# Constant lag of the first experts' result scatters, router scatters in two of three tiles, last stage with its products three steps ahead

## The chip, the cores and the metric

The kernel runs on one core of one Trainium2 chip. The core has five engines: TensorE (PE in the profile; PEld are its weight loads), VectorE (DVE), ScalarE (ACT), GpSimd (POOL) and SyncE (SP, which here only starts transfers). The metric is the device time of one execution in microseconds; lower is better.

## The reference

The input is 16 sequences of 512 tokens with 128 features, float32. A mixture of experts, an attention and the same mixture of experts again are added to it, the first and the last with the factor one half:

```python
x = L0_attn_x
x = x + 0.5 * ffn(_layernorm(x)); x = x + attn(_layernorm(x)); x = x + 0.5 * ffn(_layernorm(x))

def ffn(x):                      # top 2 of 8 experts, and a shared one
    normed = (xt - mu) * rsqrt(var + eps) * ln_gamma + ln_beta
    probs = softmax(normed @ router_w.T);  top_v, top_i = top_k(probs, 2);  gates = softmax(top_v)
    out = sum over the two chosen experts e of gate_e * swiglu(normed, gate_up_w[e], down_w[e])
    return out + swiglu(normed, shared_gate_up_w, shared_down_w)
# swiglu(h, gu, down) = (silu(h @ gate.T) * (h @ up.T)) @ down.T
```

The attention has 16 heads of 8 features and a relative position term. All of its work stands between the two places that are changed.

## The kernel before

The 8192 tokens lie in SBUF all the time as `XR`, 64 groups of 128 tokens; four groups are a step (16 steps). The program has four blocks, each ended by a barrier over all engines: `route` (routing and the experts of the first mixture), `combine`, `attention` (attention, with routing of the second mixture, and then its experts) and `finish`.

**Experts (route and attention).** POOL scatters the normalized rows to a table in HBM, `dispatched`, sorted by expert (indirect DMAs, 128 rows each). Then 71 tiles (`ET`) of 256 rows are worked off. SP loads a tile's rows up to eight tiles ahead. PE transposes them (`s_tx`), ACT copies them out, DVE splits them in high and low parts (the cast to `Xh`, L636 and L1814, is one per tile), PE makes gate and up products (`x_gu`), ACT the silu, DVE the product, PE the down product (`x_dn`), DVE copies the result out (`s_y`, L650 and L1825), and POOL scatters it with two indirect DMAs to `expert_out` in HBM (L400 and L1421). The order within each engine is the order in which the code is written; an engine goes on when the semaphores of its next instruction are there. The result buffers form a ring of 24 tiles.

POOL's scatters of tile n are bound to PE's progress. In the attention block the first waits for the gate and up products of tile n + 2 (`x_gu` at n + 3), the second for the transposes of tile n + 4. In `route` the number 3 was `lag = max(3, 15 - n // 4)`: 15 tiles at first, one less every fourth tile, 3 from tile 48 on:

```python
                q, y, lag = n % 4, n % YR, max(3, 15 - n // 4)
                    if g == 0:
                        pool.wait_ge(x_gu, min(ET, n + lag))
                    else:
                        pool.wait_ge(s_tx, min(ET, n + lag + 2))
```

In the attention block POOL also has 16 router scatters left for the last two batches (`send`, L1408). From tile `LATE` = 13 on it put one between a tile's two result scatters, in 16 tiles in a row. SP waits for all of them before it loads the rows of tile 48 and later.

**The end of the attention block.** POOL waits until its scatters have landed (L1472), and so does SP (L1355), which then loads the experts' results of steps 0 and 1 (L1359). Behind each engine's last instruction the block has a drain (L1161 in the profile) and then the barrier.

**The last stage (finish), per step.** SP loads both experts' results (`Y`, two DMAs of 256 KB, L2064). POOL scales one and adds the residual (L2082, L2084). ACT normalizes three groups (L2128) and DVE the fourth (L2091). PE transposes them (L2149), ACT applies gamma and beta (L2136), PE makes the shared expert's gate (L2158) and up (L2159), ACT the silu (L2140), DVE the hidden product (L2103), PE the down product (L2164). DVE adds the gated results (four instructions, L2098, "gated sum") and then the shared expert's (L2108), and SP stores the step (L2074). PE's down product follows its gate product by one step; `h` has two buffers.

Of the kernel before, what the change touches and what calls it, by code (L numbers as in the profile page):

```python
# [12 lines left out]
ALU = mybir.AluOpType  # L13
# [3 lines left out]
P = 128  # L17
# [127 lines left out]
def build(nc, T):  # L145
    with ExitStack() as top:
# [47 lines left out]
        with ExitStack() as c:  # L194
            R = gates(K, c, "f2", None)
            attention(K, "f2", R)
            finish(K, "f2", R)

# [19 lines left out]
def route(K, tag, R):  # L218
# [11 lines left out]
    with ExitStack() as c:  # L230
# [147 lines left out]
        def _(pool):  # L378
# [778 lines left out]
def attention(K, tag, R2):  # L1157
# [3 lines left out]
    with ExitStack() as c:  # L1161
# [94 lines left out]
        s_st = [SX(f"out{q}") for q in range(4)]  # L1256
# [34 lines left out]
        def _(sp):  # L1291
# [62 lines left out]
            for q in range(4):  # L1354
                sp.wait_ge(s_st[q], 16 * NG2 * ((ET - q + 3) // 4))  # L1355
            yv = yd[0:TOPK * TOK, :].rearrange("(k n p) d -> p k n d", k=TOPK, p=P)
            for s in range(2):
                for k in range(TOPK):
                    sp.dma_start(R2["Y"][s][k], yv[:, k, tokens(s), :]).then_inc(R2["s_ga"][s], 16)  # L1359

        @block.gpsimd
        def _(pool):
# [108 lines left out]
            for q in range(4):  # L1471
                pool.wait_ge(s_st[q], 16 * NG2 * ((ET - q + 3) // 4))  # L1472
# [560 lines left out]
def finish(K, tag, R):  # L2033
# [6 lines left out]
    with ExitStack() as c:  # L2040
        Y = R["Y"] + [[sb(c, f"{tag}_Y{q}{k}", [P, JT, D]) for k in range(TOPK)] for q in range(2, NB)]
        xn = [sb(c, f"{tag}_xn{q}", [P, JT, D]) for q in range(3)]
        nT, sg, h = ([sb(c, f"{tag}_{x}{q}", [P, L]) for q in range(2)] for x in ("nT", "sg", "h"))
# [3 lines left out]
        s_ga = R["s_ga"]  # L2047
        s_st = S("stored")
        s_n, s_nv, s_tp, s_nT, s_gu, s_sg, s_h, s_dn, s_pa, s_cb, s_out = (
            S(x) for x in ("normed", "normed_dve", "transp", "nT", "gateup", "silu", "hidden", "down", "second", "first", "shared"))  # L2050
        block = c.enter_context(nc.Block())
        JA = JT - 1
# [5 lines left out]
        def _(sp):  # L2058
# [7 lines left out]
            for s in range(2, 5):  # L2066
                wait(sp, (s_cb, JT * (s - 3)))
                load(s)
# [18 lines left out]
        def _(dve):  # L2087
            def normalize(s):
                t = JT * s + JA
                wait(dve, (s_tp, s - 2))  # L2090
                nc.vector.tensor_scalar(xn[s % 3][:, JA, :], XR[:, t, :], rstd[:, t:t + 1], shift[:, t:t + 1], ALU.mult, ALU.add  # L2091
                                        ).then_inc(s_nv, 1)

# [7 lines left out]
            def hidden(s):  # L2101
                wait(dve, (s_sg, s + 1), (s_gu, s + 1), (s_dn, s - 1))
                nc.vector.tensor_tensor(h[s % 2][:], psU[s % 2][:], sg[s % 2][:], ALU.mult).then_inc(s_h, 1)  # L2103
# [19 lines left out]
        def _(act):  # L2123
            def normalize(s):
                wait(act, (s_tp, s - 2))
                for j in range(JA):
# [6 lines left out]
            for s in range(NB + 1):  # L2133
                if s < NB:
                    wait(act, (s_tp, s + 1), (s_gu, s - 1))
                    nc.scalar.activation(nT[s % 2][:], psT[s % 2][:], ACT.Identity, bias=bet[:], scale=gam[:]).then_inc(s_nT, 1)  # L2136
                if s >= 1:
                    b = s - 1
                    wait(act, (s_gu, b + 1), (s_h, b - 1))
                    nc.scalar.activation(sg[b % 2][:], psG[b % 2][:], ACT.Silu).then_inc(s_sg, 1)  # L2140
# [4 lines left out]
        def _(pe):  # L2145
            def transposes(s):
                wait(pe, (s_n, JA * (s + 1)), (s_nv, s + 1), (s_nT, s - 1))
# [5 lines left out]
            for s in range(NB + 1):  # L2153
                if s + 1 < NB:
                    transposes(s + 1)
                if s < NB:
                    wait(pe, (s_nT, s + 1), (s_sg, s - 1), (s_h, s - 1))
                    nc.tensor.matmul(psG[s % 2][:], sgT[:], nT[s % 2][:], start=True, stop=True)  # L2158
                    nc.tensor.matmul(psU[s % 2][:], suT[:], nT[s % 2][:], start=True, stop=True).then_inc(s_gu, 1)  # L2159
                if s >= 1:  # L2160
                    b = s - 1
                    wait(pe, (s_h, b + 1), (s_out, b - 1))
                    for j in range(JT):
                        m = nc.tensor.matmul(psY[b % 2][:, j, :], h[b % 2][:, j * P:(j + 1) * P], sdT[:], start=True, stop=True)  # L2164
# [51 lines left out]
```

## Time and profile before

| | us |
|---|---|
| median of 3 runs (lowest to highest) | 2274.42 (2271.9 to 2279.68) |
| profiled execution | 2267.75 |
| its span | 2265.8 |
| first experts, 71 tiles | about 217 to 506 |
| second experts, 71 tiles | about 1885 to 2182 |
| last stage | 2197.4 to 2265.8 |

TensorE is busy 2055.6 us of the span (91%), DVE 1849.0 (82%), ACT 1351.1 (60%), POOL 1336.5 (59%). These are means over stages with different limits. In the first experts' stage TensorE sets the pace where it is busy all of a window; in the last stage DVE is the engine that is hardly idle.

### The profile page before, as it was taken

The page shows a single profiled execution, that of the slowest core. Times are in us where ns is not written, and L with a number is a line of the kernel's source. Part 1 is how long each engine was busy: PE and PEld are TensorE (multiplying, and loading weights), DVE is VectorE, ACT ScalarE, POOL GpSimd, SP SyncE. Part 2 cuts the span into 40 slices and gives each one's busy share as a digit, 9 for nine tenths or more (in the row PEclk, how much of TensorE's full clock was granted, in tenths as well). Part 3 has the DMA queues.
Part 4 walks back from the last instruction along what each step waited for, and adds up shares of the span by engine and source line. Part 5 has one row for each costly group of instructions (what it writes and reads, how often), then busy time and mean ns, then how long its engine had stood idle before and what let it go on. Part 6 is the DMA issues. An engine that isn't in the chain of part 4 may idle for free. (4 is left out here: it accounts for less than half of the span.)

```text
span 2265.8 us, 64247 instructions
## 1 busy us (share of the span) xinstructions
PE 2055.6 (91%) x22864; PEld 1244.0 (55%) x22865; DVE 1849.0 (82%) x3842; ACT 1351.1 (60%) x3301; POOL 1336.5 (59%) x1961
## 2 busy tenths in 40 slices
PE   7664988996799999999999999999999997889968
PEld 4443988893344444444444444444444447889965
DVE  6543755667699999999999999999999995666648
ACT  4332544556766766666677667667666655445545
POOL 3665155553355557757757667667577583465554
PEclk8666999999999999999999999999999999999989
DMA  5222242217801111210111011012102104232226
GB/s 158 75 67 84 64 151 88 73 50 232 209 13 34 34 26 19 45 34 13 43 34 45 11 38 49 4 39 48 34 12 44 40 24 156 60 89 74 68 63 185
DMA packets 161414, 149.02 MB, mean 66 GB/s; under 512 B 51602, under 2 KB 135698, under 8 KB 160594
## 3 DMA queue, kind: packets, MB, share of 16 engines
q1 hardware_dynamic: 141984, 109.36, 18.6%
q0 software_dynamic: 17280, 35.56, 4.8%
q8 instruction: 163, 2.67, 0.5%
q14 instruction: 113, 0.93, 0.1%
q10 hardware_dynamic: 1874, 0.51, 0.1%
HBM read 86.76 MB, written 62.55 MB: 66 GB/s over the span
## 5 line engine op out<-in xcount | busy, mean ns | idle before, releaser
L1521 PE MATMUL ps_scores<-c_relw,arena_stats 64*64 64x512 f32 x4096 | 956.5, 598 | 0.0
L1972 ACT ACTIVATE arena_probs<-ps_scores,neg_max 128x512 f32<-128x512 f32 x1024 | 697.0, 684 | 393.6 <-DVE neg_max L1857 389.7
L1857 DVE TENSOR_REDUCE neg_max<-ps_scores 128x1 f32<-128x512 f32 x1024 | 650.0, 662 | 26.9 <-PE ps_scores L1521 24.6
L1509 PE MATMUL ps_scores<-arena_rows,arena_stats 64*64 64x512 f32 x2048 | 483.6, 598 | 5.6 <-ACT arena_probs L1972 3.7
L1509 PE MATMUL ps_scores<-c_batch,arena_stats 64*64 64x512 f32 x2048 | 475.3, 596 | 4.7 <-POOL arena_stats L1449 2.6
L1521 PEld LDWEIGHTS ps_scores<-c_relw,arena_stats 64*64 64x64 f32 x4096 | 277.0, 132 | 247.3 <-issue 185.1
L1654 DVE STREAM_TRANSPOSE arena_weights<-arena_probs 128x1024 f32<-128x1024 f32 x256 | 313.5, 1224 | 1.8 <-ACT arena_probs L1972 1.8
L1654 DVE STREAM_TRANSPOSE arena_results<-arena_probs 128x1024 f32<-128x1024 f32 x256 | 313.2, 1224 | 0.0
L1447 POOL TENSOR_TENSOR arena_stats<-arena_rows,c_mask 128x128 f32<-128x128 f32 x256 | 121.9, 476 | 193.2 <-PE ps_scores L1521 191.6
L1447 POOL TENSOR_TENSOR arena_stats<-c_batch,c_mask 128x128 f32<-128x128 f32 x256 | 121.5, 475 | 193.5 <-PE ps_scores L1521 192.3
L1421 POOL DMA_INDIRECT expert_out<-arena_results,f2x_to x142 | 139.4, 982 | 120.8 <-PE ps_scores L1577 73.7
L1972 ACT ACTIVATION_READ_ACCUMULATOR arena_probs<-ps_scores,neg_max 128x1 f32 x1024 | 200.3, 196 | 0.0
L1509 PEld LDWEIGHTS ps_scores<-c_batch,arena_stats 64*64 64x64 f32 x2048 | 136.2, 132 | 106.8 <-issue 86.4
L1509 PEld LDWEIGHTS ps_scores<-arena_rows,arena_stats 64*64 64x64 f32 x2048 | 132.1, 132 | 111.2 <-issue 93.4
L1373 POOL TENSOR_TENSOR row_recip<-row_sum,minus_one 128x16 f32<-128x16 f32 x64 | 186.6, 2916 | 8.2 <-ACT arena_probs L1972 8.2
L390 POOL DMA_INDIRECT dispatched<-f1d_n,f1d_idx x128 | 124.5, 973 | 90.9 <-DVE f1d_idx L542 48.9
L400 POOL DMA_INDIRECT expert_out<-f1d_n,f1x_to x94 | 91.1, 969 | 66.4 <-PE f1d_bank L955 24.2
L1588 PE MATMUL ps_values<-c_batch,arena_results 128*128 x852 | 110.9, 281 | 19.7 <-issue 10.8
L953 PE MATMUL f1d_bank<-f1x_Xh,f1x_Th 128*128 128x256 f32 x426 | 127.1, 298 | 0.2 <-issue 0.2
L1575 PE MATMUL ps_scores<-f2x_Xh,f2x_Th 128*128 128x256 f32 x426 | 126.1, 296 | 1.1 <-DVE f2x_Xl L1818 0.9
L966 PE MATMUL f1d_bank<-f_Wd,f1d_act 128*128 x852 | 108.5, 277 | 17.2 <-DVE f1d_n L650 13.5
L955 PE MATMUL f1d_bank<-f1x_Xh,f1x_Tl 128*128 128x256 f32 x426 | 121.1, 284 | 0.5 <-issue 0.5
(323 smaller groups left out, 4225.9 us busy)
## 6 DMA issues: line engine op xcount, KB each, us to landing
qkv_record<-f1c_rec SPq DMA_DIRECT2D x16, 768.0 KB, 3.9
c_batch<-dispatched SPq DMA_DIRECT2D x71, 129.0 KB
arena_rows<-dispatched SPq DMA_DIRECT2D x71, 129.0 KB
c_batch<-qkv_record SPq DMA_DIRECT2D x32, 256.0 KB
arena_rows<-qkv_record SPq DMA_DIRECT2D x32, 256.0 KB
f2c_Y<-expert_out SPq DMA_DIRECT2D x28, 256.0 KB, 3.3
c_Os<-expert_out SPq DMA_DIRECT2D x20, 256.0 KB, 4.1
f1c_Y<-expert_out SPq DMA_DIRECT2D x16, 256.0 KB, 4.3
```

Source lines behind the costliest of these rows:

```text
L390: pool.indirect_dma_start(xd, bass.IndirectOffsetOnAxis(idx[:, k, t:t + 1], 0), n0[k][s % NR][:, j, :], None).then_inc(s_sc[s % 4], 16)
L953: nc.tensor.matmul(dst, wh, Xh[q][:], start=True, stop=False)
L955: m = nc.tensor.matmul(dst, wl, Xh[q][:], start=False, stop=True)
L1373: tt(rr[:, G % 2, :], rs[:, G % 2, :], minus[:], ALU.pow).then_inc(s_rr, 1)
L1421: pool.indirect_dma_start(yd, bass.IndirectOffsetOnAxis(to[y][:, g:g + 1], 0), Ys[y][:, g, :], None).then_inc(s_st[q], 16)
L1447: tt(SK[u % NS], qk, mk, ALU.mult).then_inc(s_ex, 1)
L1509: m = nc.tensor.matmul(out, SK[n // 2 % NS][p, h, :, :].rearrange("p h a -> p (h a)"), KT[q][p, h, :], start=True, stop=False)
L1521: m = nc.tensor.matmul(out, SR[n // 2 % NS][p, h, :, :].rearrange("p h a -> p (h a)"), R[p, w0:w0 + L], start=False, stop=True)
L1575: nc.tensor.matmul(dst, wh, Xh[q][:], start=True, stop=False)
L1654: nc.vector.transpose(PT[G % 2][:, :, 2 * pair:2 * pair + 2, :, :].rearrange("p r i h a -> p r (i h a)"), Pr[U % NPAIR].rearrange("p i (r ...
L1857: reduce_max(nmx[U % NPAIR][:, n % 2:n % 2 + 1], psS[U % NPAIR][n % 2][:], AX, negate=True).then_inc(s_mx, 1)
L1972: nc.scalar.activation(Pr[s][:, n % 2, :], psS[s][n % 2][:], ACT.Exp, bias=nmx[s][:, n % 2:n % 2 + 1], accum_out=rs[:, G % 2, tt:tt + 1]). ...
```

## The change

`route`: the lag is 3 from the first tile. `attention`: the 16 router scatters go into two of every three tiles; POOL and SP no longer wait at its end for the result scatters, and SP no longer loads steps 0 and 1 there. The semaphores of these scatters now live on into `finish`, where SP waits for them behind the barrier and then loads all steps. `finish`: ACT normalizes all four groups, `h` has four buffers, PE's down product is three steps behind its gate product, and DVE makes the hidden products three steps ahead. The small buffers lie in one piece, `early`.

```diff
@@ route, POOL @@
-                q, y, lag = n % 4, n % YR, max(3, 15 - n // 4)
+                q, y = n % 4, n % YR
-                        pool.wait_ge(x_gu, min(ET, n + lag))
+                        pool.wait_ge(x_gu, min(ET, n + 3))
-                        pool.wait_ge(s_tx, min(ET, n + lag + 2))
+                        pool.wait_ge(s_tx, min(ET, n + 5))
@@ attention, SP @@
-            for q in range(4):
-                sp.wait_ge(s_st[q], 16 * NG2 * ((ET - q + 3) // 4))
-            yv = yd[0:TOPK * TOK, :].rearrange("(k n p) d -> p k n d", k=TOPK, p=P)
-            for s in range(2):
-                for k in range(TOPK):
-                    sp.dma_start(R2["Y"][s][k], yv[:, k, tokens(s), :]).then_inc(R2["s_ga"][s], 16)
@@ attention, POOL @@
-                        if 0 <= n - LATE < TOPK * JP:
-                            send(LASTP, n - LATE)
+                        at = n - LATE
+                        if at >= 0 and at % 3 < 2 and at // 3 * 2 + at % 3 < TOPK * JP:
+                            send(LASTP, at // 3 * 2 + at % 3)
-            for q in range(4):
-                pool.wait_ge(s_st[q], 16 * NG2 * ((ET - q + 3) // 4))
@@ finish @@
-        JA = JT - 1
+        HB, AHEAD_H, ROWS = 4, 3, TR // P
@@ finish, SP @@
-            for s in range(2, 5):
+            for q in range(4):
+                sp.wait_ge(s_rows[q], 16 * ROWS * ((ET - q + 3) // 4))
+            for s in range(5):
                 wait(sp, (s_cb, JT * (s - 3)))
                 load(s)
@@ finish, DVE @@
-            for s in range(2):
-                normalize(s)
-            for s in range(NB + 1):
-                if s + 2 < NB:
-                    normalize(s + 2)
-                if s < NB:
-                    hidden(s)
-                    gated(s)
-                if s >= 1:
-                    shared(s - 1)
+            for s in range(AHEAD_H):
+                hidden(s)
+            for s in range(NB):
+                gated(s)
+                if s + AHEAD_H < NB:
+                    hidden(s + AHEAD_H)
+                shared(s)
@@ finish, ACT @@
-                for j in range(JA):
+                for j in range(JT):
@@ finish, PE @@
-            for s in range(NB + 1):
+            for s in range(NB + AHEAD_H):
-                if s >= 1:
-                    b = s - 1
+                if s >= AHEAD_H:
+                    b = s - AHEAD_H
                     wait(pe, (s_h, b + 1), (s_out, b - 1))
```

In `route` no instruction changes its place, only what it waits for. POOL in the second experts' stage, from tile 13's first result scatter (`expert_out`) on, before; `dispatched` is a router scatter:

```order
L1421 DMA expert_out<-arena_results,f2x_to 20224x128
L1408 DMA dispatched<-f_n,f_idx 69376x129
L1421 DMA expert_out<-arena_results,f2x_to 20224x128 x2
L1408 DMA dispatched<-f_n,f_idx 69376x129
L1421 DMA expert_out<-arena_results,f2x_to 20224x128 x2
```

The same place now:

```order
L1417 DMA expert_out<-arena_results,f2x_to 20224x128
L1403 DMA dispatched<-f_n,f_idx 69376x129
L1417 DMA expert_out<-arena_results,f2x_to 20224x128 x2
L1403 DMA dispatched<-f_n,f_idx 69376x129
L1417 DMA expert_out<-arena_results,f2x_to 20224x128 x4
```

After every second router scatter there are now four result scatters instead of two.

SP from the last row load of the experts to the loads of the last stage, before (`f2x_out` counts landed result scatters):

```order
L1304 DMA arena_rows<-dispatched 128x2x129
L1359 DMA c_Os<-expert_out 128x4x128 [waits f2x_out2,f2x_out3,f2x_out1,f2x_out0]
L1359 DMA c_Os<-expert_out 128x4x128 x3
L1161 UNCONDITIONAL_BRANCH
L2057 UNCONDITIONAL_BRANCH [waits barrier_Pool_Activation_PE_DVE_SP_release]
L2064 DMA f2c_Y<-expert_out 128x4x128 x4
```

The same place now:

```order
L1305 DMA arena_rows<-dispatched 128x2x129
L1162 UNCONDITIONAL_BRANCH
L2054 UNCONDITIONAL_BRANCH [waits barrier_Pool_Activation_PE_DVE_SP_release]
L2061 DMA c_Os<-expert_out 128x4x128 [waits f2x_out2,f2x_out3,f2x_out1,f2x_out0]
L2061 DMA c_Os<-expert_out 128x4x128 x3
L2061 DMA f2c_Y<-expert_out 128x4x128 x4
```

The wait for the scatters and the four loads have moved behind the barrier.

DVE at the start of the last stage, before (`xn` is the fourth group's normalization, `h` the hidden product):

```order
L2091 TENSOR_SCALAR f2c_xn<-residual,c_rs,c_shift 128x128 x3
L2103 TENSOR_TENSOR f2c_h<-f2c_psup,f2c_sg 128x512
L2098 SCALAR_TENSOR_TENSOR c_Os<-c_Os,f_gate 128x128 x4
L2091 TENSOR_SCALAR f2c_xn<-residual,c_rs,c_shift 128x128
L2103 TENSOR_TENSOR f2c_h<-f2c_psup,f2c_sg 128x512
```

The same place now (`early` holds the hidden tiles):

```order
L2096 TENSOR_TENSOR f2c_early<-f2c_psup,f2c_early 128x512 x3
L2091 SCALAR_TENSOR_TENSOR c_Os<-c_Os,f_gate 128x128 x4
L2096 TENSOR_TENSOR f2c_early<-f2c_psup,f2c_early 128x512
L2101 SCALAR_TENSOR_TENSOR c_Os<-f2c_psY,c_Os 128x512
L2091 SCALAR_TENSOR_TENSOR c_Os<-c_Os,f_gate 128x128 x4
```

Three hidden products stand ahead of the first gated sum, and DVE's normalizations are gone.

## Rows read from the trace of the kernel before

**Rows 1.** Windows of all engines: us, busy (x instructions), PE clock, DMA share, GB/s.

```profile
227.00:256.00 29.00, 29.00 (x253) 29.00 (x252) 24.46 (x78) 16.48 (x31) 0.00 (x0) 1.00 0.20 52
...
286.00:440.00 154.00, 137.08 (x1132) 133.61 (x1131) 89.76 (x246) 72.47 (x141) 91.08 (x95) 0.99 0.32 105
...
440.00:498.00 58.00, 58.00 (x504) 58.00 (x503) 40.27 (x112) 33.11 (x64) 30.65 (x32) 1.00 0.19 56
...
2230.00:2251.00 21.00, 18.66 (x97) 12.53 (x96) 20.84 (x43) 14.56 (x31) 12.94 (x12) 1.00 0.75 220
```

**Rows 2.** Windows, the first experts' casts alone (L636, one per tile).

```profile
286.00:439.80 153.80, 10.28 (x35) 0.99 0.32 105
439.80:498.30 58.50, 4.70 (x16) 1.00 0.19 56
```

**Rows 3.** Windows of the second experts' stage: all engines, then casts alone (L1814).

```profile
1962.00:2034.00 72.00, 60.24 (x484) 56.77 (x483) 44.05 (x131) 31.40 (x61) 45.05 (x47) 1.00 0.29 85
...
1962.00:2034.00 72.00, 4.48 (x16) 1.00 0.29 85
...
2040.00:2178.00 138.00, 10.90 (x37) 1.00 0.22 65
```

**Rows 4.** Timeline of one slow tile: start us, us, engine line op [idle before].

```profile
1986.19 0.42 DVE L1825 COPY arena_results<-ps_values 128x256 f32<-128x256 f32 x1 [1.01 <-remote]
...
1986.48 0.95 POOL L1421 DMA_INDIRECT expert_out<-arena_results,f2x_to  x1 [1.15 <-PE ps_scores L1577]
...
1987.74 0.96 POOL L1421 DMA_INDIRECT expert_out<-arena_results,f2x_to  x1 [0.30 <-issue]
...
1988.31 0.38 PE L1560 MATMUL ps_side<-ident,arena_rows 128*128 128x128 f32 x2
...
1989.00 0.96 POOL L1408 DMA_INDIRECT dispatched<-f_n,f_idx  x1 [0.31 <-issue]
...
1990.84 0.42 DVE L1825 COPY arena_results<-ps_values 128x256 f32<-128x256 f32 x1 [1.02 <-remote]
```

**Rows 5.** The barriers: POOL's last scatter, its two drains, ACT's first.

```profile
2185.67 0.96 POOL L1421 DMA_INDIRECT expert_out<-arena_results,f2x_to  x1 [0.30 <-issue]
...
L1161 POOLq DRAIN  x1: 8971/8971/8971, 2188.2 to 2188.2; - x1
...
L230 POOLq DRAIN  x1: 2844/2844/2844, 513.0 to 513.0; - x1
...
2197.47 1.65 ACT L2128 ACTIVATE f2c_xn<-residual,c_shift,c_rs 128x128 f32<-128x128 f32 x4 [16.44 <-PEq L1161]
```

**Rows 6.** Timeline: the first hidden product, two waits, DVE's last instructions.

```profile
2205.13 0.69 DVE L2103 TENSOR_TENSOR f2c_h<-f2c_psup,f2c_sg 128x512 f32<-128x512 f32 x1 [4.20 <-ACT f2c_sg L2140]
...
2211.68 1.04 POOL L2082 TENSOR_TENSOR f2c_Y<-f2c_Y,f_gate 128x512 f32<-128x512 f32 x1 [4.80 <-DMA f2c_Y<-expert_out]
...
2217.56 0.81 PE L2149 MATMUL f2c_psT<-ident,f2c_xn 128*128 128x128 f32 x4 [3.10 <-issue]
...
2261.48 1.28 DVE L2108 SCALAR_TENSOR_TENSOR f2c_Y<-f2c_psY,f2c_Y 128x512 f32<-128x512 f32 x2
```

**Rows 7.** Groups of 2230:2251 (busy, mean ns), then L2098, L2082, L2084 (ns).

```profile
L2098 DVE SCALAR_TENSOR_TENSOR f2c_Y<-f2c_Y,f_gate 128x128 f32<-128x128 f32 x25 | 12.8, 569 | 0.0
...
L2128 ACT ACTIVATE f2c_xn<-residual,c_shift,c_rs 128x128 f32<-128x128 f32 x18 | 7.5, 483 | 0.0
...
L2091 DVE TENSOR_SCALAR f2c_xn<-residual,c_rs,c_shift 128x128 f32<-128x128 f32 x6 | 2.2, 374 | 0.0
...
L2098 DVE SCALAR_TENSOR_TENSOR f2c_Y<-f2c_Y,f_gate x56: 336/342/1426, 2211.8 to 2261.2; 128x128 f32<-128x128 f32 x56
...
L2082 POOL TENSOR_TENSOR f2c_Y<-f2c_Y,f_gate x14: 1038/1040/1221, 2202.2 to 2253.0; 128x512 f32<-128x512 f32 x14
...
L2084 POOL TENSOR_TENSOR f2c_Y<-f2c_Y,residual x14: 1262/1268/1289, 2203.3 to 2254.1; 128x512 f32<-128x512 f32 x14
```

**Rows 8.** The page's DMA issues: count, KB each, median us to landing.

```profile
f2c_Y<-expert_out SPq DMA_DIRECT2D x28, 256.0 KB, 3.3
```

More of the change, by code:

```diff
@@ L195, in build @@
             R = gates(K, c, "f2", None)
+            R["s_st"] = [c.enter_context(nc.semaphore(f"f2x_out{q}")) for q in range(4)]
             attention(K, "f2", R)
@@ L1255, in attention @@
         s_ld = [SX(f"in{q}") for q in range(4)]
-        s_st = [SX(f"out{q}") for q in range(4)]
+        s_st = R2["s_st"]
         s_tx, s_xf, s_hl, x_gu, x_sg, x_h, x_dn, s_y, s_wl, s_to = (
@@ L2040, in finish @@
     with ExitStack() as c:
+        early = sb(c, f"{tag}_early", [P, 11 * L])
+        homes = [early[:, q * L:(q + 1) * L] for q in range(11)]
+        xn = [home.rearrange("p (j d) -> p j d", j=JT) for home in homes[0:3]]
+        nT, sg, h = homes[3:5], homes[5:7], homes[7:11]
+        assert 11 * L * 4 <= 49152
         Y = R["Y"] + [[sb(c, f"{tag}_Y{q}{k}", [P, JT, D]) for k in range(TOPK)] for q in range(2, NB)]
-        xn = [sb(c, f"{tag}_xn{q}", [P, JT, D]) for q in range(3)]
-        nT, sg, h = ([sb(c, f"{tag}_{x}{q}", [P, L]) for q in range(2)] for x in ("nT", "sg", "h"))
         psT, psG, psU = ([ps(c, f"{tag}_ps{x}{q}", [P, L]) for q in range(2)] for x in ("T", "gate", "up"))
@@ L2046, in finish @@
         S = Sems(nc, c, tag)
-        s_ga = R["s_ga"]
+        s_ga, s_rows = R["s_ga"], R["s_st"]
         s_st = S("stored")
-        s_n, s_nv, s_tp, s_nT, s_gu, s_sg, s_h, s_dn, s_pa, s_cb, s_out = (
-            S(x) for x in ("normed", "normed_dve", "transp", "nT", "gateup", "silu", "hidden", "down", "second", "first", "shared"))
+        s_n, s_tp, s_nT, s_gu, s_sg, s_h, s_dn, s_pa, s_cb, s_out = (
+            S(x) for x in ("normed", "transp", "nT", "gateup", "silu", "hidden", "down", "second", "first", "shared"))
         block = c.enter_context(nc.Block())
-        JA = JT - 1
+        HB, AHEAD_H, ROWS = 4, 3, TR // P
         def tokens(s):
@@ L2087, in _ @@
         def _(dve):
[L2088 to L2092, printed above, removed]
             def gated(s):
@@ L2101, in hidden @@
             def hidden(s):
-                wait(dve, (s_sg, s + 1), (s_gu, s + 1), (s_dn, s - 1))
-                nc.vector.tensor_tensor(h[s % 2][:], psU[s % 2][:], sg[s % 2][:], ALU.mult).then_inc(s_h, 1)
+                wait(dve, (s_sg, s + 1), (s_gu, s + 1), (s_dn, s + 1 - HB))
+                nc.vector.tensor_tensor(h[s % HB], psU[s % 2][:], sg[s % 2], ALU.mult).then_inc(s_h, 1)
             def shared(s):
@@ L2135, in _ @@
                     wait(act, (s_tp, s + 1), (s_gu, s - 1))
-                    nc.scalar.activation(nT[s % 2][:], psT[s % 2][:], ACT.Identity, bias=bet[:], scale=gam[:]).then_inc(s_nT, 1)
+                    nc.scalar.activation(nT[s % 2], psT[s % 2][:], ACT.Identity, bias=bet[:], scale=gam[:]).then_inc(s_nT, 1)
                 if s >= 1:
@@ L2139, in _ @@
                     wait(act, (s_gu, b + 1), (s_h, b - 1))
-                    nc.scalar.activation(sg[b % 2][:], psG[b % 2][:], ACT.Silu).then_inc(s_sg, 1)
+                    nc.scalar.activation(sg[b % 2], psG[b % 2][:], ACT.Silu).then_inc(s_sg, 1)
                 if s + 2 < NB:
@@ L2146, in transposes @@
             def transposes(s):
-                wait(pe, (s_n, JA * (s + 1)), (s_nv, s + 1), (s_nT, s - 1))
+                wait(pe, (s_n, JT * (s + 1)), (s_nT, s - 1))
                 for j in range(JT):
```

6 lines of the change are left out of this document (3 added, 3 removed).

## The prediction

> **What bounds the kernel now.** I read the windows by stage first, then the starts of one instruction per tile, then the wait rows, and last the end of the program. The attention middle keeps TensorE (PE) busy and the change does not touch it, so only three places matter.
>
> *First experts' stage, tiles 19 to 54.* The window 286 to 440 us has PE busy 137.08 of 154 us, while 227 to 256 and 440 to 498 have it busy all the time [rows 1]. VectorE (DVE) casts each tile's rows once, so its casts count tiles: 35 in 153.8 us, 4.39 us each, then 16 in 58.5 us, 3.66 us each [rows 2]. What differs is GpSimd (POOL). It issues 95 scatters in the slow window, 2.7 a tile, and 32 in the fast one, 2 a tile [rows 1], because its lag of 15 tiles shrinks by one tile every fourth, so it does four tiles' scatters while PE does three.
>
> *Second experts' stage.* The same again: 16 tiles in 72 us with 47 scatters, three each (two results, one router scatter), and 37 tiles in 138 us (3.73 us) where the code has two each [rows 3]. The rows of one slow tile show how it costs [rows 4]. Three scatters start at 1986.48, 1987.74 and 1989.00. PE's transposes are over at 1988.69 and the down matmuls of which the DVE copy waits came before them, yet the copy starts only at 1990.84, 1.84 us after the third scatter began. PE's signals are passed on late behind a run of three scatters. Why, the rows do not say; the price is the difference: this tile's copy starts 4.65 us after the one before it (1986.19), a free one 3.71, so 0.94 us for each third scatter.
>
> *The end.* POOL's last scatter starts at 2185.67. What then holds the block's barrier is POOL's drain, 8.971 us from 2188.2; ACT starts at 2197.47, so the barrier opens at about 2197.4. The same drain took 2.844 us behind the first experts [rows 5]. Then the last stage runs 68.4 us to the span's end at 2265.8. In its middle (2230 to 2251) DVE is busy 20.84 of 21 us over six steps, so a step is 3.50 us and DVE is its limit [rows 1, 7].
>
> **The first experts' scatters, three tiles behind.** With a constant lag POOL starts at tile 3 and issues two scatters a tile throughout. The 35 slow tiles then go at the fast pace. I take 3.70 us, between the 3.66 of [rows 2] and the 3.73 of [rows 3]: 153.8 - 35 x 3.70 = 24.3 us gained, all on the path, since PE bounds the stage and the tail (lag 3 from tile 48 on) is the same in both. Nothing is queued on POOL at that point: it is idle in the window 227 to 256 [rows 1]. The 24 scatters that move to tiles 3 to 14 come beside DVE at 24.46 of 29 us [rows 1], the only place with this rate that the trace does not show. Bounds: nothing there, and 3.66 us a tile, gives 25.7; every one of these 12 tiles held at 0.94 us gives 24.3 - 11.3 = 13.0.
>
> **The 16 router scatters of the second stage, in two of three tiles.** There are still 16 tiles with a third scatter, spread over 23. If each costs 0.94 us, nothing changes: 15.0 before and after. The first stage's regime had the same eight scatters in three tiles and cost (3 x 4.39 - 3 x 3.71) / 2 = 1.0 us for each extra one, so +1 us at worst. If POOL's rate were the limit instead (4.65 / 3 = 1.55 us a scatter), 62 scatters take 96.1 us against 23 x 3.71 = 85.3, that is 10.8 in place of 15.0, a gain of 4.2. I take 0, by the row nearest in kind. The row loads that wait for the last of these start at tile 41, three tiles behind the last send's turn, so they stay hidden.
>
> **The barrier.** POOL no longer waits for its scatters to land, so its drain starts at 2186.65 instead of 2188.2. With the same 8.97 us the barrier opens 1.6 us sooner. If the drain ends when it ended before, 0; if it takes the 2.844 us of the other block, 7.7. I take 1.6. SP's four loads of steps 0 and 1, which lay under the drain, now come behind the barrier. They land in 3.3 us [rows 8] and POOL needs 2.3 us for a step's two operations (1040 and 1268 ns [rows 7]), so step 0 is ready for DVE some 6 us behind it. What hides that is the new order itself: DVE now makes three hidden tiles before its first gated sum.
>
> **The last stage.** The first hidden tile started 7.7 us after the barrier (2205.13) [rows 6]. ScalarE (ACT) now makes the fourth normalization of a step too, two of them before its first product: +0.8. It is busy 14.56 us in six steps [rows 1], 2.4 a step, and with one more at 0.4 it needs 2.8 (18 normalizations took 7.5 us [rows 7]). So the third hidden tile ends at 7.7 + 0.8 + 2 x 2.8 + 0.6 = 14.7 us, and here the first gated sum starts. Before, it started at 8.3: the lookahead costs 6 us at the front. From there DVE has per step 3.50 less the removed normalization (2.2 us in six, 0.37 each [rows 7]) = 3.13; PE was busy 18.66 us in six steps, 3.1 each [rows 1]. The first four steps find POOL ahead and follow PE at 3.1 (12.4 us; no load is awaited, for four steps' loads go out at once, where before POOL stood 4.80 us until 2211.68 for one, and PE 3.10 us until 2217.56 [rows 6]), nine go at 3.15 (28.4), the last three have no hidden tile and a free POOL, 1.9 each (5.7), and from DVE's last operation to the end 3.0 us as now (2262.8 to 2265.8 [rows 6]). Sum 14.7 + 12.4 + 28.4 + 5.7 + 3.0 = 64.2 against 68.4: 4.2 gained. Bounds: a front of 13.0 (ACT at 2.4 a step) and 13 steps at PE's 3.1 give 62.0 (6.4 gained); all 13 steps at today's 3.50, because loads and stores are the limit at the 220 GB/s of [rows 1], give 68.9 (0.5 lost).
>
> How much POOL slows DVE decides the 3.13. A gated sum takes 336 ns at best and up to 1426 [rows 7], just over POOL's 1268, and 25 of them took 12.8 us, 2.05 a step, not 1.1. I keep the 2.05, since POOL's work for a step is not touched. Were POOL's part gone, a DVE step would be 2.2 and PE's 3.1 would bound nine steps, 0.5 us less in the sum. The Trainium skill, "SBUF — State Buffer", section "Who interferes with whom", says that a VectorE instruction with two SBUF inputs and a GpSimd one that reads SBUF exclude each other for the whole instruction. The trace agrees: the longest gated sum is 1090 ns over the shortest, about one POOL operation. By this rule the sum stays at 64.2; if POOL's work cost DVE nothing, it would be 63.7.
>
> **Sum.** 24.3 + 0 + 1.6 + 4.2 = 30.1 us. The profiled execution took 2267.75 us with a span of 2265.8; it goes to about 2237.7. The median of the runs is 2274.42, 6.7 above it, and I carry that over: **2244.3 us**.
>
> **Rivals.**
> - *Early tiles are held as well* (12%). Two scatters beside a fuller DVE hold PE's signals in tiles 3 to 14: 13.0 + 5.8 gained, 2255.6. For it: the one place without a row. Against it: the fast windows have the same pair of scatters and PE busy throughout.
> - *The drain shrinks* (8%). 2.844 us as behind the first experts: 24.3 + 7.7 + 4.2, 2238.2. For it: one of two drains measured. Against: the code behind and ahead of this barrier is unchanged.
> - *The last stage gives nothing* (11%): DMA-bound steps and the 6 us front: 24.3 - 0.5, 2250.6. For it: 0.75 of the DMA engines' time in the middle. Against: the loads now run four steps ahead.
> - *The slow window was never about scatters* (4%), but say the DMA traffic, 105 GB/s there against 52 and 56 [rows 1]. Then only the 5.8 us at the end are left: 2268.6, no change. Against: the second stage slows the same way with three scatters at 85 GB/s [rows 3], and there the extra traffic is the third scatter's own.
> - *Slower* (3%): two scatters a tile hold PE's signals wherever DVE is late, in all of tiles 3 to 54. Each held tile costs 0.94, so 52 cost 48.9 against the 24.3 + 5.8 taken away: 2293.2. It decides from 33 held tiles on. Against: tiles 55 to 70 and 37 tiles of the second stage show none.
>
> **How the numbers follow.** The likeliest case holds 62%, with its own range 2239 to 2250. The 80% range leaves out the slower case, most of the no-change one and the tail of a short drain: 2235 to 2257. A measurement of this kernel can tell 0.3%, 6.8 us: faster 0.93 (the likeliest and the first three rivals), within 0.3% 0.04, slower 0.03.
>
> **What would show it.** Right: casts in the first experts' stage at 3.7 us from tile 5 to 70, no scatter run longer than two there, PE busy all of 240 to 495 us; second stage's slow stretch as long in sum; POOL's drain near 9 us; three hidden tiles before the first gated sum, steps of about 3.1 us, stage near 64 us. Wrong: casts beyond 4 us apart with two scatters a tile, or a last stage as long as 68 us.

## The result, and the profile after

The changed kernel took 2248.19 us (median of 4 runs, 2248.01 to 2249.22) against 2276.82 for the kernel before (4 runs, 2271.9 to 2279.68): a ratio of 0.9877, 95% interval 0.9857 to 0.9898, or 28.6 us. Forecast was 2244.3 us. The two profiled executions differ by less, 2265.8 to 2246.2 us of span, 19.6 us: the one of before (2267.75 us) was 4.2 us shorter than the shortest of its timed runs, and the one of after (2248.01 us) is an average one. The sections below count with the traces first and come back to the rest.

**First experts' stage.** The windows of the cast that stands once in each tile (L637 now), answering to [rows 2]; columns are the window, its length, DVE's time in this line with its count, PE clock, DMA share, GB/s:

```profile
291.40:421.20 129.80, 10.30 (x35) 1.00 0.35 111
226.60:291.40 64.80, 4.98 (x17) 0.94 0.30 90
421.20:480.70 59.50, 4.86 (x17) 1.00 0.19 57
```

The 35 tiles that took 153.8 us take 129.8, 3.71 each. All engines in the same window (PE, PEld, DVE, ACT, POOL), answering to the slow window of [rows 1]:

```profile
291.40:421.20 129.80, 129.80 (x1123) 129.80 (x1122) 88.73 (x245) 72.16 (x140) 67.32 (x70) 1.00 0.35 111
```

PE is never idle, and POOL issues 70 scatters, two a tile. Not all of the 24 us is kept. Tile 2 starts at 226.7 in place of 224.3, ahead of anything that the lag could move, and from tile 2 to tile 19 the starts of the cast stand 64.8 us apart, where they stood 62.1 apart before. These 2.7 us lie in tiles 2 to 5 alone; from tile 5 on the pace is the same as before, with two scatters a tile. All engines in tiles 2 and 3 now, and in tile 2 before:

```profile
226.70:231.50 4.80, 3.94 (x16) 3.43 (x17) 3.16 (x12) 2.06 (x4) 0.00 (x0) 0.50 0.19 50
231.50:235.70 4.20, 4.20 (x29) 4.20 (x28) 3.31 (x13) 2.17 (x4) 1.49 (x2) 0.70 0.41 110
```

```profile
224.30:227.70 3.40, 3.40 (x32) 3.40 (x31) 3.06 (x12) 2.12 (x4) 0.00 (x0) 1.00 0.29 83
```

Tile 2 runs at the low level of PE's granted clock (0.50, 1.2 GHz); before, the clock was at the high one (1.00, 2.4 GHz) there. In the 7.6 us ahead of tile 2 PE was busy 2.93 us now and all the time before. The first result scatter starts at 233.38, behind tile 2, so at least 1.4 of the 2.7 us are not the new lag's.

**Second experts' stage.** The 23 tiles from tile 17 to tile 40, before and after, all engines:

```profile
1961.60:2061.90 100.30, 88.54 (x728) 85.07 (x728) 64.65 (x187) 47.76 (x92) 60.38 (x62) 1.00 0.28 82
```

```profile
1944.10:2045.30 101.20, 89.21 (x735) 85.93 (x735) 64.62 (x186) 48.37 (x92) 60.28 (x62) 1.00 0.28 81
```

The same 62 scatters in nearly the same time, however they are spread. The other first-chip traces of the next section widen this: 102.6 and 103.8 us with the old order (end_only, lag_only), 100.8 and 100.9 with the new one (router_only, fours).

**The barrier.** POOL's last scatter, its drain (ns) and ACT's first instruction, answering to [rows 5]:

```profile
2167.86 0.95 POOL L1417 DMA_INDIRECT expert_out<-arena_results,f2x_to  x1 [0.30 <-issue]
...
L1162 POOLq DRAIN  x1: 11198/11198/11198, 2166.1 to 2166.1; - x1
...
2177.57 0.88 ACT L2118 ACTIVATE f2c_early<-residual,c_shift,c_rs 128x128 f32<-128x128 f32 x2 [14.34 <-PEq L1162]
```

The drain now reads 11.2 us because it is entered before the last scatters have run; it ends at 2177.3, 9.4 us after the last scatter started. Before it ended at 2197.2, 11.5 us after. That is 2.1 us gained. In the other traces from this chip it ends 11.5 and 11.1 us after that start with POOL's wait for the landings (lag_only, router_only), and 9.9 and 9.5 without it (end_only, fours).

**The last stage.** From the end of the drain to the end of the span it takes 68.9 us, and took 68.6. DVE's first hidden tile and first gated sums (start, us, engine, line, idle before):

```profile
2185.57 0.69 DVE L2096 TENSOR_TENSOR f2c_early<-f2c_psup,f2c_early 128x512 f32<-128x512 f32 x1 [19.31 <-ACT f2c_early L2130]
...
2191.54 1.13 DVE L2091 SCALAR_TENSOR_TENSOR c_Os<-c_Os,f_gate 128x128 f32<-128x128 f32 x4
...
2236.83 2.14 DVE L2091 SCALAR_TENSOR_TENSOR f2c_Y<-f2c_Y,f_gate 128x128 f32<-128x128 f32 x4
```

The order is the planned one: three hidden tiles, then the first gated sum 14.2 us behind the barrier. The row at 2236.83 is the fourteenth step's gated sums, so 13 steps took 45.3 us, 3.48 each. In parts, by the starts of the gated sums (us, from the end of the drain):

| | before | after |
|---|---|---|
| to the first gated sum | 8.5 | 14.2 |
| the first 4 steps | 16.3 | 13.1 |
| the next 9 steps | 32.6 | 32.2 |
| from there to the end | 11.2 | 9.4 |

The later front is paid back, all but 0.3 us, by the first four steps, which now find hidden tiles ready, and by the end. The nine steps between, 3.63 us each before and 3.58 now, are about as long as they were, although each has lost a normalization. The groups of 2210 to 2231 (line, busy us, mean ns), answering to [rows 7], show where it went:

```profile
L2091 DVE SCALAR_TENSOR_TENSOR f2c_Y<-f2c_Y,f_gate 128x128 f32<-128x128 f32 x24 | 15.7, 711 | 0.0
```

A gated sum takes 711 ns, and took 569. By the traces the parts of the 19.6 us are: +23.7 in tiles 19 to 54, -2.4 at tile 2, -2.7 from there to tile 19, -0.7 behind tile 54, -0.3 from there to the second experts' last tile, +2.3 up to the barrier (2.1 of it behind the last scatter) and -0.3 in the last stage, 19.6 in all.

### The profile page after: what moved, and what is told of

It reads as the page before. It is cut to its first block and busy times, and to the rows that moved or that the text cites. A ratio compares the mean times of both kernels' runs of the same rounds, so it can differ in the third digit from the quotient of the medians.

```text
span 2246.2 us, 64242 instructions
## 1 busy us (share of the span) xinstructions
PE 2052.5 (91%) x22864; PEld 1242.0 (55%) x22865; DVE 1844.7 (82%) x3826; ACT 1356.8 (60%) x3317; POOL 1336.8 (60%) x1961
## 5 line engine op out<-in xcount | busy, mean ns | idle before, releaser
L1582 PE MATMUL ps_values<-c_batch,arena_results 128*128 x852 | 111.2, 281 | 19.6 <-DVE arena_results L1819 10.8
L955 PE MATMUL f1d_bank<-f1x_Xl,f1x_Th 128*128 128x256 f32 x426 | 121.6, 285 | 0.0
```

Source lines behind the costliest of these rows:

```text
L955: nc.tensor.matmul(dst, wh, Xl[q][:], start=False, stop=False)
```

## The experiments

They ran in three sets, and each set beside runs of the kernel before on its own chip. That turned out to matter: before took 2275.5 us in the first set, like the result's 2276.8, but 2131.7 and 2131.8 in the second and third. Ratios are within a set.

### Set one: which part of the change gives the time

**lag_only** is the kernel before with this alone:

```
-                q, y, lag = n % 4, n % YR, max(3, 15 - n // 4)
+                q, y = n % 4, n % YR
...
-                        pool.wait_ge(x_gu, min(ET, n + lag))
+                        pool.wait_ge(x_gu, min(ET, n + 3))
...
-                        pool.wait_ge(s_tx, min(ET, n + lag + 2))
+                        pool.wait_ge(s_tx, min(ET, n + 5))
```

> The kernel before with only the first experts' lag set to three tiles. My theory (a third scatter back to back holds PE's signals, about 2 us for each of the runs of four in tiles 19 to 54): the whole of the stage's gain is here, 18 us by the two profiles shown and up to the 24 predicted, so 2250 to 2257 us, and the casts of tiles 19 to 54 stand 3.7 us apart. Rival (the gain is mostly in the end of the program or in the router scatters): under 5 us.

2253.6 us (2252.02 to 2255.18), ratio 0.9899 (0.9881 to 0.9917), 21.9 us of 2275.5. Its casts of tiles 19 to 54:

```profile
291.20:420.90 129.70, 10.30 (x35) 1.00 0.34 111
```

**end_only** is the changed kernel with the lag and the router scatters of before, so it has the missing wait at the end of attention, the loads moved and the new last stage.

> The changed kernel with the first experts' lag and the router scatters as before: only the end of the attention block and the last stage are changed. By the profiles: about 2 us from the barrier (POOL's landing wait gone, drain as long as it was) and nothing from the last stage (68.7 us against 68.4), so 0.998 to 1.000 of the time before. The prediction's own terms were 1.6 + 4.2 = 5.8 us. Rival (the last stage gains and the trace of after is an odd one): 6 us and a last stage of 64 us.

2272.99 us, ratio 0.9989 (0.9975 to 1.0002), 2.5 us and not clear of zero. The last stage is 68.6 us again, and the casts of tiles 19 to 54, with the old lag, are slow:

```profile
290.70:442.90 152.20, 10.69 (x35) 1.00 0.33 105
```

**router_only** is the kernel before with this alone:

```
-                        if 0 <= n - LATE < TOPK * JP:
-                            send(LASTP, n - LATE)
+                        at = n - LATE
+                        if at >= 0 and at % 3 < 2 and at // 3 * 2 + at % 3 < TOPK * JP:
+                            send(LASTP, at // 3 * 2 + at % 3)
```

> The kernel before with only the router scatters sent in two of three tiles. If each third scatter costs its own 0.94 us: no change, casts over tiles 17 to 40 in 100 us, as one stretch of 16 slow and 7 free tiles was. Rival (POOL's rate is the limit, so that spreading pays): 4 us faster. Rival (a tile behind two crowded ones loses too): 2 to 4 us slower.

2273.49 us, ratio 0.9992 (0.9982 to 1.0002): no change that can be told, and tiles 17 to 40 took 100.8 us. A loss of 2 to 4 us is excluded by the interval; a gain of 4 us lies at its very edge (0.9982 is 4.1 us). The parts give 21.9, 2.5 and 2.0, in all 26.4 of the 28.6 us, and only the first is clear of zero: the lag is about four fifths of the change.

**fours** changes only when POOL issues the two-a-tile scatters of the changed kernel:

```
-                    if g == 0:
-                        pool.wait_ge(x_gu, min(ET, n + 3))
-                    else:
-                        pool.wait_ge(s_tx, min(ET, n + 5))
+                    if n % 2 == 0 and g == 0:
+                        pool.wait_ge(x_gu, min(ET, n + 4))
+                        pool.wait_ge(s_tx, min(ET, n + 6))
```

> The changed kernel, but in the first experts' stage POOL waits until both tiles of a pair are due and then issues their four scatters in one run: still two a tile, but runs of four instead of two. If runs of three and more hold PE's signals, each run costs what the run of four cost in the slow window of before, 3 x (4.39 - 3.71) = 2.0 us, so 33 runs cost 60 to 70 us and the program takes about 2310. Rival (only the rate counts, 2.7 scatters a tile were too many for POOL or the DMA): no loss, 2248.

2300.07 us in one run, 52 above the changed kernel. So on this chip it is the run of scatters and not their rate. Its timeline (start, us, engine, line, idle before):

```profile
329.25 0.96 POOL L400 DMA_INDIRECT expert_out<-f1d_n,f1x_to  x1 [4.36 <-DVE f1d_n L650]
...
330.51 0.96 POOL L400 DMA_INDIRECT expert_out<-f1d_n,f1x_to  x1 [0.30 <-issue]
...
331.78 0.96 POOL L400 DMA_INDIRECT expert_out<-f1d_n,f1x_to  x1 [0.30 <-issue]
...
333.04 0.96 POOL L400 DMA_INDIRECT expert_out<-f1d_n,f1x_to  x1 [0.31 <-issue]
335.01 0.42 DVE L650 COPY f1d_n<-f1d_bank 128x256 f32<-128x256 f32 x1 [2.73 <-remote]
335.06 0.56 ACT L820 ACTIVATE c_batch<-f1d_bank,beta_col,gamma_col 128x256 f32<-128x256 f32 x1 [2.82 <-remote]
...
335.69 1.60 PE L966 MATMUL f1d_bank<-f_Wd,f1d_act 128*128 x12 [1.40 <-DVE f1d_n L650]
```

DVE and ACT, which both wait for PE, start together 1.97 and 2.02 us after the fourth scatter began, and then PE waits for DVE. In tiles 19 to 54 (the casts L636 here) the stage took 160.4 us, so a pair of tiles costs 1.7 us more than with runs of two, where 2.0 were expected:

```profile
302.30:462.70 160.40, 10.29 (x35) 1.00 0.29 93
```

### Set two: the last stage

Four variants of the changed kernel, to find what keeps the step at 3.5 us. **dve_norm** gives DVE the fourth normalization back (not shown: the first five of them ahead of the loop, ACT's loop over three groups, PE's wait for both):

```
+            def normalize(s):
+                t = JT * s + JT - 1
+                wait(dve, (s_tp, s - 2))
+                nc.vector.tensor_scalar(xn[s % 3][:, JT - 1, :], XR[:, t, :], rstd[:, t:t + 1], shift[:, t:t + 1], ALU.mult, ALU.add
+                                        ).then_inc(s_nv, 1)
...
                gated(s)
+                if s + AHEAD_H + 2 < NB:
+                    normalize(s + AHEAD_H + 2)
```

> The changed kernel, but DVE makes the fourth normalization of each step again, as before; the order with three hidden tiles ahead stays. The last stage of the changed kernel took 68.9 us from the end of POOL's drain, at 3.5 us a step, though DVE lost 0.37 us of work a step: its gated sums went from 2.05 to 2.6 us a step. Theory 1 (a gated sum and a POOL operation, both on SBUF alone, do not run together: a step is POOL's 2.31 plus the gated sums' 1.13, 3.44 us, and DVE's other work fits beside POOL's): the stage becomes at most 1 to 2 us longer. Theory 2 (DVE's own sum of work bounds the step and the 0.37 was really saved, something else having grown): 13 steps of 0.37, 4 to 5 us longer.

**quarter** and **half** move one or two of a step's four token tiles from POOL to DVE (JG is 3 or 2; not shown: POOL's operations over JG tiles only, and DVE's wait for POOL, which now stands behind these lines):

```
+                for j in range(JG, JT):
+                    t = JT * s + j
+                    nc.vector.scalar_tensor_tensor(out=Y[s][1][:, j, :], in0=Y[s][1][:, j, :], scalar=G2[:, t:t + 1],
+                                                   in1=XR[:, t, :], op0=ALU.mult, op1=ALU.add).then_inc(s_pd, 1)
```

> The changed kernel, but of each step's four token tiles in the last stage one is multiplied and added by DVE (one more operation of 0.3 us a step) and POOL keeps three. Theory 1 (POOL's operations and the gated sums exclude each other): 1.73 of POOL plus 1.43 of DVE is 3.16 a step in place of 3.44, the stage 3 to 4 us shorter. Theory 2 (DVE's work is the sum, POOL's share of the slowing fixed): 0.3 us a step longer, 4 to 5 us. Theory 3 (loads and stores at 217 GB/s bound the step): no change, 3.5 us a step.

> The same with two of four token tiles moved from POOL to DVE. Theory 1: 1.16 of POOL plus 1.73 of DVE exclude each other, 2.9; DVE alone needs 3.1 and PE 3.1, so the step is 3.1 to 3.2 and the stage 4 to 5 us shorter than 68.9. Theory 2: 8 to 9 us longer. Theory 3: no change.

**ahead1** has one hidden tile ahead:

```
-        HB, AHEAD_H, ROWS = 4, 3, TR // P
+        HB, AHEAD_H, ROWS = 4, 1, TR // P
```

> The changed kernel, but with one hidden tile made ahead in place of three; ACT still normalizes all four. The first gated sum starts some 6 us earlier (8 us behind the barrier in place of 14). If the step stays bound by POOL and the gated sums at 3.5 us, that time comes back but for the waits the lookahead hid: the stage 2 to 6 us shorter than 68.9. If the lookahead is what keeps PE and DVE supplied (my prediction): the steps get longer and the stage stays at 68 to 69 us.

Medians 2130.30, 2129.98, 2129.72 and 2127.14 us; ratios to before 0.9994 (0.9985 to 1.0004), 0.9990 (0.9980 to 1.0000), 0.9987 (0.9977 to 0.9997) and 0.9980 (0.9971 to 0.9990). From the end of the drain to the end the stage took 69.9, 69.8, 69.7 and 66.4 us; the changed kernel's own on these chips is 69.4 (set three). dve_norm is 0.5 us longer in all, and not 4 to 5. This is a sum of two: ACT, with less to do, lets the first gated sum start 1.9 us sooner, and the first four steps take 2.1 us more. The nine steps behind them take 32.6 us against 32.5 in the changed kernel (set three), and they are the test: a normalization more on DVE costs nothing there, as theory 1 has it. Taking POOL's work away and giving it to DVE costs nothing, and gains nothing either. Theory 1 had 3 to 5 us here and is missed; no change is what theory 3 forecast, and set three tries that. In half DVE's additional operation took 576 ns, not 300, in spite of the smaller POOL part, and PE was busy 20.62 of 21 us:

```profile
2085.00:2106.00 21.00, 20.62 (x104) 13.63 (x103) 20.38 (x51) 18.36 (x40) 8.24 (x12) 1.00 0.78 227
```

```profile
L2091 DVE SCALAR_TENSOR_TENSOR f2c_Y<-f2c_Y,f_gate,residual 128x128 f32<-128x128 f32 x12 | 6.4, 576 | 0.0
```

ahead1 is the best of the complete kernels here. Its first gated sum starts 5.4 us sooner than in the changed kernel. The first four steps, without hidden tiles in store, take 16.2 us in place of 12.9, the nine behind them 30.8 in place of 32.5, and the end 0.7 more. Expected was that longer steps would take the whole of the 5.4 us back; the steps and the end took 2.4.

### Set three: before and after on such a chip, POOL gone, the DMA loaded

**before_again** and **after_again** are the two kernels themselves.

> The kernel before, unchanged, profiled beside the next three. The four kernels of the last comparison ran on another chip, where before took 2131.7 us and the kernels with the new lag 2127 to 2130: there the traces show three and four scatters back to back with casts still 3.7 us apart. If that is the chip, this kernel there has no slow window in tiles 19 to 54 (35 tiles in about 130 us) though its lag still shrinks; on the first chip it has one (151 to 158 us). Rival (the gain was never from the lag): the slow window is there and the changed kernel lacks it, with the same total.

> The changed kernel, unchanged, as the base of the last stage on the same chip. From the end of POOL's drain to the end 68.9 us on the first chip. If chips don't differ in this stage: 68.9 here too. Against before: 0.9877 on the first chip; where runs of scatters hold nothing, only the barrier is left, 2 us, 0.999.

**no_pool** leaves out, for the last stage, POOL's two operations and DVE's wait for them (not shown), so the second gate and the residual are missing from its result:

```
-                nc.gpsimd.tensor_tensor(y, y, G2[:, tokens(s)].unsqueeze(2).broadcast_to([P, JT, D]), ALU.mult).then_inc(s_pa, 1)
-                wait(pool, (s_pa, 2 * s + 1))
-                nc.gpsimd.tensor_tensor(y, y, XR[:, tokens(s), :], ALU.add).then_inc(s_pa, 1)
```

> The changed kernel with POOL's two operations a step left out of the last stage (the second gate and the residual are not applied). Theory 1 (POOL's operations stretch DVE's gated sums): gated sums 0.34 us each, DVE needs 2.5 us a step, PE 3.1, so the step falls from 3.5 to 3.1 and the stage by 5 us. Theory 3 (loads and stores of 768 KB a step at 220 GB/s bound it): the step stays at 3.5 and DVE waits for loads.

**extra_store** writes each result twice (not shown: the last wait counts both):

```
                 sp.dma_start(ov[:, tokens(s), :], Y[s][1][:]).then_inc(s_st, 16)
+                sp.dma_start(xv2[:, tokens(s), :], Y[s][1][:]).then_inc(s_st, 16)
```

> The changed kernel with each step's result stored a second time, to another place in memory: 1024 KB a step in place of 768. Theory 3 (the DMA's rate bounds the step): 3.5 becomes 4.6 us and the stage 13 to 17 us longer. Theory 1 (POOL and DVE bound it, the DMA engines at three quarters have room): at most 2 us, for the last store.

The kernel before took 2130.98 us, the changed one 2129.88: ratios to the shared runs of before 1.0001 (0.9992 to 1.0011) and 0.9991 (0.9982 to 1.0001). The change that gave 28.6 us gives 1 to 2 here, and not clear of zero. The casts of tiles 19 to 54 in before_again, and all engines in the same window:

```profile
194.20:323.90 129.70, 11.55 (x35) 1.00 0.43 138
```

```profile
194.20:323.90 129.70, 129.70 (x1122) 129.70 (x1121) 90.88 (x246) 74.49 (x141) 99.11 (x100) 1.00 0.43 138
```

The old lag, 100 scatters in 35 tiles, more DMA traffic than on the first chip, and no loss: 129.7 us, as with the new lag. One piece of its timeline:

```profile
254.65 0.96 POOL L400 DMA_INDIRECT expert_out<-c_Os,f1x_to  x1 [0.30 <-issue]
...
255.91 0.95 POOL L400 DMA_INDIRECT expert_out<-c_Os,f1x_to  x1 [0.30 <-issue]
...
256.84 0.41 DVE L650 COPY f1d_n<-f1d_bank 128x256 f32<-128x256 f32 x1
257.17 1.14 POOL L400 DMA_INDIRECT expert_out<-c_Os,f1x_to  x1 [0.30 <-issue]
...
258.61 0.96 POOL L400 DMA_INDIRECT expert_out<-c_Os,f1x_to  x1 [0.30 <-issue]
...
259.88 0.96 POOL L400 DMA_INDIRECT expert_out<-c_Os,f1x_to  x1 [0.30 <-issue]
...
260.54 0.42 DVE L650 COPY f1d_n<-f1d_bank 128x256 f32<-128x256 f32 x1
261.14 0.96 POOL L400 DMA_INDIRECT expert_out<-c_Os,f1x_to  x1 [0.30 <-DVE f1d_n L650]
```

Six scatters back to back, with DVE's copies 3.70 us apart in the middle of them. The same instructions of POOL, the same 0.96 us and 1.26 us apart, as on the first chip, and PE's signals come through. The second stage's three scatters a tile cost nothing either: its 23 tiles from 17 to 40 take 84.1 us, where the first chip needs 100 to 103.

The last stage: windows of 2085 to 2106 of after_again, no_pool and extra_store in this order, with PE, PEld, DVE, ACT and POOL,

```profile
2085.00:2106.00 21.00, 19.82 (x107) 13.52 (x106) 21.00 (x37) 17.66 (x38) 13.15 (x13) 1.00 0.77 225
```

```profile
2085.00:2106.00 21.00, 21.00 (x112) 14.44 (x111) 16.02 (x43) 18.52 (x40) 0.00 (x0) 1.00 0.90 263
```

```profile
2085.00:2106.00 21.00, 21.00 (x113) 14.48 (x112) 20.86 (x38) 18.38 (x39) 14.11 (x12) 1.00 1.15 304
```

and the groups of DVE in the same window, of before_again, after_again and no_pool:

```profile
L2098 DVE SCALAR_TENSOR_TENSOR f2c_Y<-f2c_Y,f_gate 128x128 f32<-128x128 f32 x24 | 10.1, 481 | 0.0
L2091 DVE TENSOR_SCALAR f2c_xn<-residual,c_rs,c_shift 128x128 f32<-128x128 f32 x6 | 4.5, 746 | 0.0
```

```profile
L2091 DVE SCALAR_TENSOR_TENSOR f2c_Y<-f2c_Y,f_gate 128x128 f32<-128x128 f32 x24 | 14.6, 666 | 0.0
```

```profile
L2086 DVE SCALAR_TENSOR_TENSOR f2c_Y<-f2c_Y,f_gate 128x128 f32<-128x128 f32 x28 | 7.9, 344 | 0.0
```

Without POOL's work the gated sums take 344 ns, PE is busy all the time with a step of 3.0 us, the stage takes 61.9 us in place of 69.4 and the program 2122.18 (2120.39 to 2122.33). The DMA moves the same bytes a step at 263 GB/s there, and 304 GB/s with a third more bytes a step, so 225 is not its limit. In extra_store the stage grows by 4.9 us to 74.3 and the program to 2134.11 us; the last hidden tile even starts sooner (55.4 us behind the drain against 58.9), and what is longer is the end: 7.9 us from DVE's last operation to the end in place of 2.7. Theory 3 had 13 to 17 us, theory 1 at most 2. In before_again the operations of DVE that run on SBUF alone took 10.1 + 4.5 = 14.6 us in this window with the normalization, and in after_again 14.6 without it. DVE was busy 20.39 and 21.00 of the 21 us and both windows hold six steps, so equal sums alone would prove little; that the time hangs on POOL is shown by no_pool.

## Why the prediction was right where it was, and wrong where it was not

*First experts, 24.3 us.* Right in place, mechanism and size of the slow window: the 35 tiles gave 23.7 in the trace, and lag_only gave 21.9 over whole runs. fours is the test of "PE's signals are passed on late behind a run of three scatters": the rate unchanged, the run of four brought back, and the hold with it. The step on tiles 3 to 14 was taken at nothing, with 11.3 us as its bound. Between tiles 2 and 19 after lost 2.7 us and lag_only 3.8 (65.9 us) against the 62.1 of before, but router_only, which has the old lag, took 64.8 and end_only 62.7. In each of them the excess lies in tiles 2 to 5, where PE's granted clock was low (in tile 2 0.50 in after and lag_only, 0.54 in end_only, 0.80 in router_only); from tile 5 on all go at the pace of before. So the rival "early tiles are held as well" is false. Whether the new lag adds to the loss in tiles 3 and 4 is open.

*Router scatters, 0.* Right within what the runs can tell: 100.3 to 103.8 us for the 23 tiles in three traces with the old order, 100.8 to 101.2 in three with the new one, and no difference by runs. A gain of 1 to 3 us is not excluded.

*The barrier, 1.6.* 2.1 by the two traces of before and after on the first chip (11.5 to 9.4 us from the last scatter's start), and the same on the third (11.5 to 9.5); the other first-chip pairs give 1.1 to 2.1. The drain did not shrink to the 2.8 us of the other block. Why it takes 9 us here was not tried.

*The last stage, 4.2.* Wrong. "From there DVE has per step 3.50 less the removed normalization" failed, and the sentence under it, "I keep the 2.05, since POOL's work for a step is not touched". The front came out (14.2 for 14.7) and the tail (9.4 for 8.7); the 13 steps took 45.3 us, not 40.8. The first four, which were to follow PE, took 13.1 for 12.4, and the nine behind them 32.2 for 28.4, 3.58 us each in place of 3.15: here is the error. The gated sums did not keep 2.05 us a step, they went to 2.6. The prediction had read the stretching of the gated sums rightly, as an exclusion with POOL, and the runs show that; but it booked it as a fixed surcharge. What DVE spends waiting belongs to POOL's operations, not to DVE's list: taken off one instruction it falls on the next that uses SBUF alone. Before, the normalization was one of those (746 ns in before_again; 374 in the shown window of before [rows 7], where the gated sums and it took 12.8 + 2.2 = 15.0 us and the gated sums alone take 15.7 now). "Were POOL's part gone", the text said, the sum would be 0.5 us less; no_pool showed 7.5. It forecast 63.7 us for the stage without POOL, and 61.9 were measured: what it had wrong was POOL's price. This also makes the rival "the last stage gives nothing" true in its number (68.9 us forecast, 68.9 measured), for another reason than it gave: not the DMA, which moved up to 304 GB/s, but POOL. (Its 2250.6 also forgets the barrier's 1.6; with it, 24.3 + 1.6 - 0.5 gives 2249.0.)

*The exclusion rule.* The Trainium skill's rule of "SBUF — State Buffer", "Who interferes with whom", which stood beside the sum as if it left it unchanged, agrees with the change from 666 to 344 ns when POOL's work is gone. Used as a bound, it would have changed the sum: 2.31 us of POOL and 1.13 of gated sums, not at once, is 3.44 a step where 3.15 was taken, and 3.58 was measured. It does not give the timing, though: quarter and half should have come to 3.1 or 3.2 by it, and the traces have 3.46 and 3.43 between hidden tiles. In half DVE, PE and ACT are all busy for 87 to 98% of the time and POOL's operations still fall on DVE's. Why that is not better is open.

*The sum.* 30.1 forecast, 28.6 by medians. That the two are so near is luck. By the traces the change gave 19.6 us, 10.5 less than the 30.1: 4.5 in the last stage, 5.1 up to tile 19, the rest in small pieces. Against this stands the "6.7 above it, and I carry that over", which was wrong by 6.5 the other way: the profiled run of after is only 0.2 us under its median. The two errors leave 3.9 us, 2244.3 forecast and 2248.19 measured. Where the 6.7 us come from is read from three traces and not tried; they seem to be made in the slow places on this chip: tile 2 starts at 224.3 in the profiled before but at 228.0 and 228.2 in end_only and router_only, and the 23 tiles take 100.3 there but 102.6 in end_only. The change takes the largest of these places away, and the runs of after spread over 1.2 us where those of before spread over 7.8.

*What no part of it foresaw* is that the largest term depends on the chip, or on the state that it was in. On the chip of the third set the first two terms are zero and the change is worth about the barrier's 2 us, 0.9991 (0.9982 to 1.0001).

*A better kernel.* The lookahead of three hidden tiles costs 5.4 us at the front against a lookahead of one and gives 2.4 back, 1.7 in the steps and 0.7 at the end. With one, the stage takes 66.4 us, 3.0 less than the changed kernel's 69.4, and the program 2127.14 us (0.9980 of before, 0.9971 to 0.9990) against 2129.88 for the changed one on a chip of the same kind (0.9991, 0.9982 to 1.0001; the intervals overlap). It was not run on a chip of the first kind; its stage would be worth the same there, by the equal lengths of the stage (68.6 to 68.9 and 69.4), which is an argument and no measurement.

## What to carry to other kernels

Where many indirect scatters are issued beside work that passes signals from TensorE, look at their runs in the timeline, not at the number a tile: pairs cost nothing here, a run of three or four costs 1 to 2 us on one chip and nothing on two others, so a trace from one chip is no forecast for another. Where DVE operations on SBUF vary between 340 and 1400 ns beside POOL work, do not count their excess as DVE's own work: add POOL's time and DVE's SBUF-only time, and compare with the step. The sum is a lower bound and no forecast: in quarter and half the step stayed 0.3 to 0.5 us above it. And a profiled execution's distance to the median lies in some stage; if the change touches that stage, it is not carried over.

## What the runs showed of the hardware that was not expected

The same program, with POOL's scatters of 0.96 us every 1.26, runs in 2275 us on one chip and 2131 on two others. The traces put the difference where scatters stand in runs. The first experts' tile 0 starts at 205 to 217 us on the one and at 126 to 128 on the others; the router's scatters are issued there, 16 in a row at a time. Tiles 19 to 54 take 152 to 154 us against 129.7 with the old lag; tiles 17 to 40 of the second stage 100 to 104 against 84.1. Of the 136.9 us between the spans of before and before_again 90.0 lie ahead of tile 0, 23.8 in tiles 19 to 54, and 6.9 and 16.2 in tiles 0 to 17 and 17 to 40 of the second stage. Ahead of tile 0 the granted clock differs too (0.68 on average from 20 us to 205, against 0.86 from 20 to 126), and PE is busy 23 us longer for the same matmuls, so not all of the 90 us there are waits. In tiles 19 to 54 the clock is full on both. Where no scatters stand in runs the chips agree within 1.6 us: 1367.1 to 1368.7 us from the first barrier to the second experts, 110.5 to 111.2 us for their last 30 tiles, 68.6 to 68.9 and 69.4 for the new last stage. What holds the signals, and whether it is the chip or a state that it was in during those runs, the runs can't tell.

More bytes made the steps of the last stage shorter: 3.2 us between hidden tiles in extra_store against 3.5, with POOL and DVE doing the same work. The loads land later there (5.1 us by the median against 3.3) and POOL's operations fall elsewhere between DVE's; that this is the reason was not tried.
